# Entry norms of both batches inside the recurrence's own block, with layer 0's turned weights copied by VectorE

## The reference

```python
h = _layernorm(x, axis=-1) * (1 + ca) + sa          # modulated norm, ca and sa per batch and channel
x = x + ga * _L1_attn_ref(h, ...)                   # below
# _L1_attn_ref(x):
x = layernorm(x, ln0_w, ln0_b)
for l in range(4):
    h = layernorm(x, ln1_w[l], ln1_b[l])
    hh = time_shift(h)
    k = Wk @ (h*tmk + hh*(1-tmk));  v = Wv @ (h*tmv + hh*(1-tmv));  sr = sigmoid(Wr @ (h*tmr + hh*(1-tmr)))
    x = x + Wo @ (sr * wkv(time_decay[l], time_first[l], k, v))     # wkv: a recurrence over the 1024 tokens
    h = layernorm(x, ln2_w[l], ln2_b[l])
    ... x = x + sigmoid(Wcr @ xr) * (Wcv @ square(relu(Wck @ xk)))
```

## Time and profile before

| | us |
|---|---|
| three executions | 1102.53, 1103.72, 1227.85 (median 1103.72) |
| the profiled execution, its own time | 1098.75 |
| its span, first to last instruction | 1097.0 |
| PE busy | 1027.1 (94% of the span) |
| DVE busy | 766.0 (70%) |
| ACT busy | 584.2 (53%) |
| POOL busy | 63.4 (6%) |

### The profile page before, as it was taken

The page is one execution under the profiler, slowest core; times in us unless marked ns, Lnnn a source line. Parts: engine busy times, 40 slices in busy tenths (PEclk is TensorE's granted clock), DMA queues, the critical chain, the costliest instruction groups (busy, mean ns, idle before and its releaser), DMA issues. The chain is left out here.

```text
span 1097.0 us, 12632 instructions
## 1 busy us (share of the span) xinstructions
PE 1027.1 (94%) x3858; PEld 447.4 (41%) x3858; DVE 766.0 (70%) x1325; ACT 584.2 (53%) x909; POOL 63.4 (6%) x152
## 2 busy tenths in 40 slices
PE   6889999999889999999999998769999999998998
PEld 3543344443333444444444443324344443443433
DVE  4988888887567555555555555378889888987675
ACT  4235666667764222222222223467788778776643
POOL 1012222222110000000000000000000000000000
PEclk9899999999999999999999999779999999998999
DMA  3742112200141645465554642000001010000001
GB/s 99 225 90 52 45 43 48 49 14 11 33 98 44 134 91 133 99 131 110 117 124 103 136 104 56 10 0 23 10 1 31 1 50 1 0 1 0 1 1 38
DMA packets 49980, 64.68 MB, mean 59 GB/s; under 512 B 17570, under 2 KB 41232, under 8 KB 45328
## 3 DMA queue, kind: packets, MB, share of 16 engines
q1 hardware_dynamic: 49100, 63.28, 24.6%
q10 hardware_dynamic: 832, 0.79, 0.2%
HBM read 55.87 MB, written 5.77 MB: 56 GB/s over the span
## 5 line engine op out<-in xcount | busy, mean ns | idle before, releaser
L977 ACT ACTIVATE pt<-psum 128x1024 f32<-128x1024 f32 (+1 forms) x192 | 150.2, 814 | 105.5 <-PE psum L748 105.1
L1131 DVE TENSOR_REDUCE part_max<-psum 128x1 f32<-128x512 f32 (+3 forms) x304 | 184.2, 657 | 31.3 <-PE psum L730 19.5
L1288 DVE TENSOR_TENSOR moe_gu<-moe_silu,psum 128x512 f32<-128x512 f32 x132 | 90.7, 687 | 152.1 <-PE psum L891 147.8
L1115 ACT ACTIVATE moe_silu<-psum 128x512 f32<-128x512 f32 x112 | 66.9, 597 | 200.1 <-PE psum L886 200.1
L886 PE MATMUL psum<-h,moe_wt 128*128 128x512 f32 x264 | 135.8, 596 | 1.0 <-issue 1.0
L891 PE MATMUL psum<-h,moe_wt 128*128 128x512 f32 x264 | 135.3, 594 | 1.4 <-DVE moe_gu L1288 1.4
L896 PE MATMUL psum<-moe_hid,moe_wt 128*128 128x512 f32 x264 | 135.1, 593 | 0.7 <-DVE moe_hid L1296 0.7
L726 PE MATMUL psum<-ka,qa 72*128 72x512 bf16 (+3 forms) x384 | 113.2, 335 | 4.6 <-DVE part_max L1131 1.6
L748 PE MATMUL psum<-qa,ka 75*128 75x512 bf16 (+3 forms) x384 | 93.8, 326 | 3.1 <-DMA qa<-neg_t 2.0
L1296 DVE TENSOR_TENSOR moe_hid<-moe_gu,qa 128x512 f32<-128x512 f32 x120 | 83.1, 692 | 13.7 <-DVE moe_gu L1288 5.8
L764 PE MATMUL psum<-pt,va_g 128*32 128x512 f32 (+3 forms) x768 | 81.8, 498 | 0.5 <-POOL pt L697 0.3
(11 more groups left out here) (262 smaller groups left out, 1361.5 us busy)
## 6 DMA issues: line engine op xcount, KB each, us to landing
qa<-comb_rows SPq DMA_DIRECT2D x56, 512.0 KB, 6.2
qa<-rows_q SPq DMA_DIRECT2D x21, 192.0 KB
ka<-rows_k SPq DMA_DIRECT2D x21, 192.0 KB
o_den<-acc SPq DMA_DIRECT2D x32, 64.0 KB, 2.1
moe_raw<-in_L_ffn_eg_w SPq DMA_DIRECT2D x32, 64.0 KB, 5.5
moe_raw<-in_L_ffn_eu_w SPq DMA_DIRECT2D x32, 64.0 KB, 5.3
moe_raw<-in_L_ffn_ed_w SPq DMA_DIRECT2D x32, 64.0 KB, 5.1
qa<-comb_rows SPq DMA_DIRECT2D x16, 128.0 KB, 3.2
```

What stands on the lines that cost most here:

```text
L977: act.activation(pt[:, u % 4, :, 0:n], score_bank[u % 2][:, :, 0:n], ACT.Exp, scale=SCALE)\
L1115: act.activation(sg[:, c % 2, :], g_bank[:, :], ACT.Silu).then_inc(silu_done, 1)
L1131: dve.tensor_reduce(part_max[:, h0:h0 + heads, slot], bank_of("fill", f)[:, 0:heads * nk].rearrange("p (h n) -> p h n", h=heads), AX_X, AL ...
L1288: dve.tensor_tensor(gu[:, at % 2, :], sg[:, at % 2, :], u_bank[:, :], ALU.mult).then_inc(gu_done, 1)
```

## The change

`stage_rwkv_in` is gone. Its work moves to the head of the recurrence's block, beside the modulated norm of batch 1, which gets banks 4 to 7, the tile `gap` for its squares and the tile `n2` for its reciprocal deviations. The ln0 norm of batch 1 and the time norm of unit 1 move forward, to between the products of unit 0 and ahead of `body(1)`. Layer 0's turned weights are copied by DVE (`keep_a` in DVE's program) and no longer by ACT.

```diff
-def stage_rwkv_in(nc, G, A):
...
 # numbers of the norms
+        n_in = G.ln_count
+        n0 = n_in + 4
+        def ln_in(c):
+            return n0 + c if c >= 2 else n_in + 2 + c
 # sync
+                load_time_weights(sp, G, A, 0)
+                load_channel_weights(sp, G, A, 0)
 # tensor, body(u)
                     time_centre(u, 0)
+                    if u == 1:
+                        time_centre(u, 1)
                     if u % 2:
                         turn_c(l, 1)
                     time_variance(u, 0)
-                    time_centre(u, 1)
+                    if u == 1:
+                        time_variance(u, 1)
+                    else:
+                        time_centre(u, 1)
                     output(p, 0)
-                    time_variance(u, 1)
+                    if u > 1:
+                        time_variance(u, 1)
 # tensor, ahead of body(1)
+                def mod_centre(q):
+                    pe.matmul(G.bank[4 + q][:, :], G.centre[:, :], G.x[:, chunk(2 + q)], start=True, stop=True)\
+                        .then_inc(mod_centred, 1)
+                def mod_var(q):
+                    pe.wait_ge(mod_squared, q + 1)
+                    if q == 0:
+                        pe.wait_ge(a_kept, 1)
+                    pe.matmul(G.bank[6 + q][:, :], G.mean[:, :], mod_sq[q], start=True, stop=True).then_inc(mod_variance, 1)
+                def in_centre(c):
+                    pe.wait_ge(G.h_in, c + 1)
+                    ln_centre(pe, G, ln_in(c), G.h[:, chunk(c)], c % 2)
+                for q in range(2):
+                    ln_centre(pe, G, n_in + q, G.x[:, chunk(q)], q)
+                for q in range(2):
+                    ln_variance(pe, G, n_in + q, q)
+                mod_centre(0)
+                mod_centre(1)
                 turn_a(0)
+                in_centre(0)
+                in_centre(1)
+                mod_var(0)
+                ln_variance(pe, G, ln_in(0), 0)
+                ln_variance(pe, G, ln_in(1), 1)
+                mod_var(1)
                 for q in range(2):
+                    pe.wait_ge(G.r_done, q + 1)
                     time_centre(0, q)
                 for q in range(2):
                     time_variance(0, q)
+                pe.wait_ge(G.h_in, 3)
                 keys(0, 0)
+                pe.wait_ge(G.h_in, 4)
                 keys(0, 1)
+                in_centre(2)
+                in_centre(3)
                 values(0, 0)
                 values(0, 1)
+                ln_variance(pe, G, ln_in(2), 0)
+                ln_variance(pe, G, ln_in(3), 1)
                 receptance(0, 0)
                 receptance(0, 1)
...
 # scalar, body(u)
-                    square(ln_time(u, 0), 0)
+                    if u > 1:
+                        square(ln_time(u, 0), 0)
...
-                    log(ln_time(u, 0), 0)
-                    square(ln_time(u, 1), 1)
-                    rstd(ln_time(u, 0), 0)
-                    log(ln_time(u, 1), 1)
-                    rstd(ln_time(u, 1), 1)
+                    if u > 1:
+                        log(ln_time(u, 0), 0)
...
 # scalar, ahead of body(1)
-                keep_a(0)
-                norm(lambda q: ln_time(0, q))
...
+                norm(n_in)
+                mod_square(0)
+                square(ln_in(0), 0)
+                mod_square(1)
+                square(ln_in(1), 1)
+                log(ln_in(0), 0)
+                rstd(ln_in(0), 0)
+                log(ln_in(1), 1)
+                rstd(ln_in(1), 1)
+                mod_rstds(0)
+                square(ln_time(0, 0), 0)
+                square(ln_time(0, 1), 1)
+                mod_rstds(1)
+                log(ln_time(0, 0), 0)
+                rstd(ln_time(0, 0), 0)
+                log(ln_time(0, 1), 1)
+                rstd(ln_time(0, 1), 1)
+                keep_k(0, 0)
+                keep_k(0, 1)
+                square(ln_in(2), 0)
+                square(ln_in(3), 1)
+                keep_v(0, 0)
                 decay(0, "e2b", e2b, 1.0)
+                keep_v(0, 1)
                 decay(0, "e1b", e1b, -1.0)
+                log(ln_in(2), 0)
+                rstd(ln_in(2), 0)
+                log(ln_in(3), 1)
+                rstd(ln_in(3), 1)
                 decay(0, "e1", e1, -1.0)
                 decay(0, "e2", e2, 1.0)
                 sigmoids(0)
+                for q in range(2):
+                    square(ln_time(1, q), q)
+                for q in range(2):
+                    log(ln_time(1, q), q)
+                    rstd(ln_time(1, q), q)
 # vector, body(u)
+                    if u == 1:
+                        time_scale(u, 0)
+                        time_bias(u, 0)
                     residual(p, 0)
-                    time_scale(u, 0)
-                    time_bias(u, 0)
+                    if u > 1:
+                        time_scale(u, 0)
+                        time_bias(u, 0)
 # vector, ahead of body(1)
+                def keep_a():
+                    dve.wait_ge(a_turned, 1)
+                    for i in range(3):
+                        turned = G.bank[6][:, chunk(i, P)]
+                        dve.tensor_scalar(wt_a[0][:, 2 * i, :], turned, vec(TMK + i, 0), None, ALU.mult)
+                        dve.tensor_scalar(wt_a[0][:, 2 * i + 1, :], turned, rest[:, 4 * i:4 * i + 1], None, ALU.mult)
+                    dve.tensor_copy(wt_a[0][:, WO, :], G.bank[6][:, chunk(3, P)]).then_inc(a_kept, 1)
                 for q in range(2):
-                    time_scale(0, q)
+                    enter(dve, G, n_in + q, q)
+                keep_a()
                 for q in range(2):
-                    time_bias(0, q)
+                    enter_ln0(dve, G, ln_in(q), q, G.r_done)
+                enter_mod(0)
+                enter_mod(1)
+                time_scale(0, 0)
+                time_bias(0, 0)
+                time_scale(0, 1)
+                time_bias(0, 1)
                 peak(0)
...
-                for q in range(2):
-                    enter(dve, G, n0 + 2 + q, 2 + q)
                 addend(0)
                 scans(0)
+                for q in range(2):
+                    enter_ln0(dve, G, ln_in(2 + q), 2 + q, r_new)
                 fractions(0)
-                for q in range(2):
-                    enter_ln0(dve, G, n0 + 4 + q, 2 + q, r_new)
```

More of the change, by code:

```diff
@@ L1477, in stage_rwkv @@
         r_new = mem.sem("rw_r_new")
-        n0 = G.ln_count
+        mod_centred, mod_squared, mod_variance, mod_logged, mod_rstd, mod_scaled = (
+            mem.sem(f"rw_mod_{what}") for what in ("centred", "squared", "variance", "logged", "rstd", "scaled"))
+        mod_sq = [gap[:, chunk(q)] for q in range(2)]
+        mod_rs = [n2[:, chunk(q)] for q in range(2)]
+        n_in = G.ln_count
+        n0 = n_in + 4
         banks = G.psum3
@@ L1511, in ln_last @@
         def ln_last(c):
-            return n0 + 4 * UNITS + (2, 3, 6, 7)[c]
+            return n0 + 4 * UNITS + (0, 1, 4, 5)[c]
         def seq(b, q):
@@ L1528, in ln_time @@
         def ln_time(u, q):
-            return n0 + 4 * u + (2 if u else 0) + q
+            return n0 + 4 * u + q
         def ln_channel(u, q):
-            return n0 + 4 * u + 8 + q
+            return n0 + 4 * u + 6 + q
+        def ln_in(c):
+            return n0 + c if c >= 2 else n_in + 2 + c
         def after_dve(u, name):
@@ L1884, in _ @@
                     time_variance(0, q)
+                pe.wait_ge(G.h_in, 3)
                 keys(0, 0)
+                pe.wait_ge(G.h_in, 4)
                 keys(0, 1)
+                in_centre(2)
+                in_centre(3)
                 values(0, 0)
                 values(0, 1)
+                ln_variance(pe, G, ln_in(2), 0)
+                ln_variance(pe, G, ln_in(3), 1)
                 receptance(0, 0)
                 receptance(0, 1)
-                for q in range(2):
-                    ln_centre(pe, G, n0 + 2 + q, G.x[:, chunk(2 + q)], q)
-                for q in range(2):
[L1895 to L1900, removed]
                 for u in range(1, UNITS + 1):
@@ L1933, in rstd @@
                     act.activation(G.rs[:, q, :], G.rs[:, q, :], ACT.Exp, scale=-0.5).then_inc(G.ln.rstd, 1)
[L1935 to L1940, removed]
                 def keep_k(u, q):
@@ L2066, in body @@
                     inverse(p, 1)
-                    log(ln_time(u, 0), 0)
-                    square(ln_time(u, 1), 1)
-                    rstd(ln_time(u, 0), 0)
-                    log(ln_time(u, 1), 1)
-                    rstd(ln_time(u, 1), 1)
+                    if u > 1:
+                        log(ln_time(u, 0), 0)
+                        square(ln_time(u, 1), 1)
+                        rstd(ln_time(u, 0), 0)
+                        log(ln_time(u, 1), 1)
+                        rstd(ln_time(u, 1), 1)
                     square(ln_channel(p, 0), 0)
@@ L2113, in body, with mod_square @@
                         keep_chosen(1)
-                act.wait_ge(start, 5)
```

(23 more changed lines are left out.)

7 lines of the change are left out of this document (added).

## The result

The changed kernel took 1087.95 us (median of 4 executions, 1086.46 to 1090.18), the old one beside it 1103.12 (median of 4). The ratio is 0.9876, with a 95% interval of 0.9836 to 0.9915: faster by about 1.2%, between 0.85% and 1.64%. By the ratio the gain is 13.7 us, by the medians 15.2. Against the predicted 1095.9 the median is 8 us lower, 1 us under the low end of the range; the ratio times the prediction's 1103.72 gives 1090.0, just inside it. 11 more executions of the same kernel later gave a median of 1092.62 (1086.51 to 1107.02) and a ratio of 0.9919 (0.9894 to 0.9944). The ratios leave out executions in a second, slower state, such as that of 1107.02.

A forecast was written before the change was run, and what follows sets the result against it. Before unit 1's keys a dependent chain was taken to set the time, then PE. Entry 2.8, keys 0.1, DVE's path 6.4, ACT's queue -0.8, stretch after rw -0.7 sum to 7.8: 1103.72 becomes 1095.9 us, range 1089 to 1101.5.

The forecast's parts named there:

- the opening is a dependent chain and the gain arrives whole: Before unit 1's keys a dependent chain sets the time; PE bounds the units, so earlier keys(1, 0) shortens the end equally.
- Part 1: Entry up to h: nothing changes though batch 0's norms join batch 1's; PE reaches in_centre(0) near 685.2 as before.
- Part 2: Turned weights on DVE: seven copies take 1.85 us and hold PE's variances, so r comes 1.8 us later.
- Part 3: To unit 0's keys: keys(0, 0) starts at 699.9 instead of 702.67, 2.8 us earlier.
- Part 4: Keys(0, 0) to max scan: clock low as the keys start, four products 6.4 us plus 0.9; scan at 707.2.
- rival A: PE's denser start keeps the full clock until the keys end; gain 10.7 or a little more, 1093 us; chance 0.2.
- Part 5: Max scan to gate product: DVE's path sums to 20.1 us against 26.5 before; gate product at 727.3, 9.3 earlier.
- Part 6: Gate product to rw: ACT's queue, holding unit 1's norm, delays the inverse; rw at 730.9 instead of 728.6 without it.
- Part 7: From rw to keys(1, 0): 8.2 us against 7.5 before, outputs at half clock; 6.7 if all at full clock.
- B: Rival: half clock at every norm product and through the stretch after rw; gain 2.9, 1100.8 us; chance 0.16.
- C: Rival: the second half's waits return elsewhere, only the entry's 2.8 stays and is eaten after rw; 1103.7 us; chance 0.05.
- D: Rival, slower: half clock outlasts the stretch after rw into unit 1; 1105.9 us at 20 us longer; chance 0.04.

The follow-up runs named there:

- r8: Changed kernel with unit 1's time norm back in body(1), batch 0's variances ahead of mod_var(0), mod_rstds(1) and enter_mod(1) behind unit 0's time norm; 1084.99 us.
- r10: The combined kernel (r8) with idle 128-column products in three gaps: before keys(0, 0), behind receptance(0, 1), before unit 1's first variance; 1088.52 us, ratio 0.9883.
- r11: The combined kernel (r8) run again unchanged; 1088.25 us, ratio 0.9880.
- r3: Changed kernel with seven more unused DVE copies of 128x128 from PSUM ahead of the seven real ones; 1094.79 us, ratio 0.9935.
- r2: Changed kernel with the turned-weight copies back on ACT, behind mod_square(0); 1089.9 us, ratio 0.9892.
- r5: Changed kernel with batch 0's two variances ahead of mod_var(0) in PE's queue; 1091.16 us, ratio 0.9887.
- r9: Changed kernel with idle 128-column products filling PE's gaps: 15 behind receptance(0, 1), 18 ahead of output(0, 0); 1089.29 us, ratio 0.9868.
- r4: Changed kernel with unit 1's time norm back in body(1), as in the old kernel; 1090.49 us, ratio 0.9915.
- r6: Changed second half, but both batches' entry norms in their own block, then the old barrier, transposes and ACT's copies; 1097.24 us, ratio 0.9953.
- r1: The changed kernel run again unedited, for a second profile; median 1092.62 us, ratio 0.9919.

## Why the prediction was right or wrong

**That the opening is a dependent chain and the gain arrives whole: right.** The tail behind keys(1, 0) is 350.0 to 350.3 in the first two profiles and in nine of the twelve later ones; the three others (r8, r10, r11) are the combined kernels, with 347.2, 351.4 and 348.8, of which more below.

**Part 1, h unchanged: right,** 4.41 for 4.33.

**Part 2, the copies cost 1.85 and r is 1.8 later: right.** Measured 1.84 and 14.16 - 12.32 = 1.84 from the first centre to r's last shift. r3 shows that the wait is real, r2 that ACT is 0.34 better in the same place, r5 that the order of PE's queue makes it 1.8.

**Part 3, keys(0, 0) 2.8 earlier: right,** 20.35 behind the first centre instead of 23.11.

**Part 4 is the step that failed.** "I take the clock as low when the keys start" gave 7.3 to the scan. It took 4.33, because the clock was full. This is 3.0 of the 3.5 that the sum was short, and it was rival A, with 0.2. What I had not weighed is that the clock at the keys is no property of the order: the same instructions at the same distances had it full in the two profiles of the changed kernel and in r9 (4.33), and half in r4 (7.37). The Trainium skill, TensorE: Matmul & The Clock Gate, "Part 1: The HAM clock gate", says that the number of slow products at the start of a kernel differs from run to run of that kernel. The runs show the same in the middle of one: 4.33 and 7.37 behind one order of instructions, and 6.02 for the same four products and a copy in r2, r5 and r6, behind other entries. A forecast by one value should have been a share of the two, and that the first profile had the full clock was luck to the amount of 3 us.

**Part 5, DVE's path 20.1: right,** 20.17, in every profile with this order to 0.01.

**Part 6, the queue ahead of rw: right in kind, too large.** 2.68 instead of 3.6. rw waits 1.46 for ACT's inverse. r4 shows 1.26 without the queue, and r9 1.25 with the same queue at full clock, so the wait needs both the queue and the half clock. The centres began at full clock, which fell only at 718.2, so the second logarithm came sooner than reckoned.

**Part 7: right,** 8.58 for 8.2, at half clock until window 731, and 6.76 with the gaps filled for the 6.7 reckoned at full clock.

**The sum** was 7.8 and the opening gained 11.3: +3.0 from part 4, +0.9 from part 6, -0.4 from part 7. The rest of the distance to the median lies outside the opening. The entry starts between 678.5 and 686.3 us in these profiles, with the same code ahead of it. The clock is a part of that: from the first product of layer 0's experts (L886) to the entry it is 363.5 us in five profiles with next to no half clock there, 365.0 to 365.2 in six with 3.4 us of it, 366.9 in r1 with 6.8, and 368.1 in r6 and r11 with 9.7. r9's attention stage took 278.1 us with 20.5 of half clock, against 272.0 to 273.5 with 6.8 to 11.2 in the others. What moves the start of the first attention product between 40.7 and 45.2 us was not tried and stays open. Rival A came; B, C and D didn't.

## What to carry to other kernels

When a gain is a per cent and the part ahead of it scatters by as much, measure the changed stretch by the starts of the same instructions in two profiles, not by the total, and keep apart the stretches in which the clock differs. In a sparse opening, ask of every product that waits for a slow engine what stands behind it in its queue: two lines exchanged (r5, 1.8 us) were worth more than the choice of the engine that makes the copies (r2, 0.34). Work moved forward to fill an idle engine can leave a gap that costs it its clock, so count the gaps left over as well as those closed.

## What the runs showed of the hardware

- A scaled float32 copy of 128x128 from PSUM begins every 0.258 us on VectorE and every 0.25 us on ScalarE (r2: seven from 688.39 to 690.21), though the records last 0.34 and 0.36 to 0.39. Moving such copies between the two changes whose queue holds them, and their sum by under 0.1 us.
- The half clock can be there when a stage begins: in nine of the twelve later profiles the clock stood at 1.2 GHz behind the first centre, and h came 5.75 to 6.94 us behind it instead of 4.4, for the same two norms. Layer 0's end, with the same code in all of them, leaves the clock differently from run to run.
- With idle products of 128 columns in the gaps the clock was full from the receptance to keys(1, 0) in two kernels (r9, r10), one profile of each. They shortened rw to keys(1, 0) by 1.8 us in r9 and 0.8 in r10, and no stretch from h to keys(1, 0) is longer with them.
- Two more stretches of half clock lie in the last units, in the one-microsecond windows 987 to 991 and 1001 to 1004 of the changed kernel. The old kernel has one, twice as long, and a tail of 350.1. r8 has none and 347.2, r11 one and 348.8, the changed kernel both and 350.2, r10 both, the first one longer, and 351.4. The order of the instructions there is the same in all. So the clock alone moves this kernel's time by as much as the edits under test.
